# A four-stage block on one core: the delta rule's iteration is cut into other pieces, its triangle formed one iteration ahead, and Exp and Ln share one table set in stage one

## The reference

```
# stage one, the parts that use exp and ln
delta = softplus(delta @ W_dt.T + b_dt);  deltaA = exp(delta[..., None] * -exp(A_log))
# stage three: 8 heads of 32, chunks of 32 tokens, for each batch, head and chunk:
q, k, v = silu(causal_conv4(x @ W));  q, k = l2norm(q), l2norm(k);  beta = sigmoid(x @ b_w)
attn = strict_lower(-(k * beta) @ k.T)
for i in range(1, 32):                        # the triangular solve
    attn[i, :i] += attn[i] @ attn[:, :i]
attn += I;  u = attn @ (v * beta);  w = attn @ (k * beta)
# the chain over the chunks, S is the 32x32 state of a head
u = u - w @ S;  o = q @ S + lower(q @ k.T) @ u;  S = S + k.T @ u
```

## Time and profile before

| | us |
|---|---|
| median of three runs (lowest, highest) | 2549.03 (2548.79, 2552.73) |
| the profiled execution | 2558.99 |
| its span, first to last instruction | 2557.4 |
| stage one, about | 0 to 1111 |
| stage three, first to last DVE instruction | 1384.5 to 2291.1 |

### The profile page before, as it was taken

One profiled execution on the slowest core, in us unless ns is written; L12 is line 12 of the kernel. 1 busy time (PEld: TensorE's weight loads), 2 busy tenths in 40 slices (PEclk: granted clock), 3 DMA queues, 4 the chain that ended last, 5 costly groups with the idle time before them and its releaser, 6 DMA issues. The chain is left out here.

```text
span 2557.4 us, 33988 instructions
## 1 busy us (share of the span) xinstructions
PE 1259.5 (49%) x13656; PEld 592.4 (23%) x13656; DVE 1503.6 (59%) x1992; ACT 915.0 (36%) x1547; POOL 979.6 (38%) x447
## 2 busy tenths in 40 slices
PE   4455555555555554336553343454543535354654
PEld 1112121212121211013221112233322233332222
DVE  1688888888979787943112356456464554625112
ACT  4574747564656565412101231332313313012110
POOL 0788787878787887910000000101101011020000
PEclk8667777776667776558775665676766757567776
DMA  3717171717171717058983001111121110218995
GB/s 91 164 42 181 42 181 42 181 43 181 43 181 43 169 42 169 17 196 300 382 335 104 17 25 43 27 34 26 38 55 26 34 31 22 59 50 312 355 389 196
DMA packets 205726, 311.13 MB, mean 122 GB/s; under 512 B 84944, under 2 KB 136912, under 8 KB 189200
## 3 DMA queue, kind: packets, MB, share of 16 engines
q1 hardware_dynamic: 202512, 306.54, 40.6%
q0 software_dynamic: 2048, 2.10, 0.4%
q10 hardware_dynamic: 1024, 0.53, 0.1%
HBM read 266.12 MB, written 42.99 MB: 121 GB/s over the span
## 5 line engine op out<-in xcount | busy, mean ns | idle before, releaser
L347 POOL TENSOR_TENSOR state<-dx_rep,b_rep 128x2048 f32<-128x2048 f32 x128 | 577.6, 4524 | 64.0 <-issue 49.6
L557 DVE TENSOR_TENSOR_SCAN psum<-psum,state 128x1024 f32<-128x1024 f32 x160 | 365.9, 2287 | 97.1 <-ACT psum L446 61.2
L687 PE MATMUL psum<-state,sel 128*32 128x512 f32 x1024 | 191.3, 835 | 347.8 <-POOL state L354 339.3
L446 ACT ACTIVATE psum<-delta_rep,a_neg 128x511 f32<-128x511 f32 x512 | 330.4, 680 | 67.3 <-DVE state L557 67.0
L354 POOL TENSOR_TENSOR state<-state,c_rep 128x1024 f32<-128x1024 f32 x96 | 225.7, 2351 | 126.8 <-DVE state L557 126.8
L557 DVE TENSOR_TENSOR_SCAN state<-psum,state 128x1024 f32<-128x1024 f32 x96 | 218.7, 2278 | 18.3 <-ACT psum L446 18.3
L623 PE MATMUL psum<-xt,w_in 128*128 128x512 f32 x256 | 178.9, 863 | 82.9 <-DVE delta L532 44.3
L564 DVE TENSOR_TENSOR state<-psum,c_rep 128x1024 f32<-128x1024 f32 x160 | 195.9, 1224 | 5.5
L1457 DVE TENSOR_TENSOR prod<-t_lane,n_lane 128x1 f32<-128x1 f32 (+30 forms) x248 | 134.2, 541 | 82.5 <-DMA n_lane<-n_scratch 75.2
L832 POOL DMA_DIRECT2D moe_b<-in_w x64 | 33.3, 522 | 324.1 <-DVE moe_xt L962 320.2
L1642 PE MATMUL psum<-xt_delta,w_qkv 128*128 128x512 f32 x192 | 116.5, 762 | 60.2 <-DVE conv_qkv L1445 58.8
(11 more groups left out here) (191 smaller groups left out, 2312.4 us busy)
## 6 DMA issues: line engine op xcount, KB each, us to landing
moe_w_set<-in_w SPq DMA_DIRECT2D x32, 4096.0 KB, 36.1
delta_rep<-delta_scratch SPq DMA_DIRECT2D x128, 256.0 KB, 4.5
dx_rep<-dx_scratch SPq DMA_DIRECT2D x128, 256.0 KB, 7.3
moe_x<-x_after SPq DMA_DIRECT2D x32, 512.0 KB, 8.5
b_rep<-bc_scratch SPq DMA_DIRECT2D x32, 256.0 KB, 4.8
c_rep<-bc_scratch SPq DMA_DIRECT2D x32, 256.0 KB, 7.7
delta_scratch<-delta SPq DMA_DIRECT2D x32, 256.0 KB, 2.0
dx_scratch<-delta_x SPq DMA_DIRECT2D x32, 256.0 KB, 2.4
```

Of the source, the lines that this page charges most:

```text
L347: nc.gpsimd.tensor_tensor(ring[q % RING][:, :, :], dx_rep[u % CHUNKS][:, :, :], free_bcast(b_rep[q // QPB % 2][:, g, :], 1, CB), ALU.mult) ...
L446: ins = nc.scalar.activation(dec[:, i, 1:], delta_rep[u % CHUNKS][:, c, 1:], ACT.Exp, scale=a_neg[:, dt * CB + c, g:g + 1])
L557: nc.vector.tensor_tensor_scan(bx if by_pool(k) else flat, flat, bx, 0.0, ALU.mult, ALU.add).then_inc(S["scan_done"], 1)
L687: ins = nc.tensor.matmul(bank[32 * c:32 * c + 32, :], sel[:, :], ring[q % RING][:, c, :], start=False, stop=(g == NG4 - 1), skip_group_che ...
```

## The change

In stage one ACT loads the set "natural_log_exp_and_others", which holds both Exp and Ln, ahead of `norm_root` and after each group of Silu. ACT_TABLE_LOADs in the program's list for stage one go from 78 to 33, in stage three from 33 to 17.

In stage three front is split: *conv* (unit i+2: layer norm, transposes, projections, taps) and *front* (unit i+1: Silu, statistics, gates, tokens, gram). An iteration has 16 slots and takes pieces of five stages, so of up to five units, before four; there are 12 iterations instead of 11. The triangles of a unit are formed in slots 6 to 8 of the iteration before their solve; `n_lane` and `t_lane` have two copies each. The solve's rows are spread over slots 0 to 14, conv's taps stand in slots 11, 13 and 15, the chain in slots 4 to 15. v has one buffer of its own, and all Silu of a unit stand together in slot 0. POOL scales the solved triangle in slot 3 of the iteration in which the chain reads it. SP stores the triangles ahead of the tail's store.

```diff
@@ -447,6 +447,7 @@
                                                    scale=a_neg[:, dt * CB + c, g:g + 1])
                     ins.then_inc(S["decay_ready"], 1)
 
+                nc.scalar.preload_act_table_set("natural_log_exp_and_others")
@@ -498,6 +502,7 @@
                         if i == 29:
                             z_silu(n, 2)
                             z_silu(n, 3)
+                            nc.scalar.preload_act_table_set("natural_log_exp_and_others")
...
-    SLOTS = 3 * CT
+    SLOTS = 4 + 3 * CT
-        cuts = [1, 14, 18, 22, 25, 28, C]
-        return range(cuts[m], cuts[m + 1]) if m < 6 else ()
+        cuts = [1, 9, 13, 16, 19, 21, 23, 24, 25, 26, 27, 28, 29, 30, 31, C, C]
+        return range(cuts[m], cuts[m + 1])
...
+        feats = [m_.sb(f"feat{i}", P, 2 * KD, CT, P) for i in range(COPIES)]
+        v_feat = m_.sb("v_feat", P, KD, CT, P)
...
-        n_lane = m_.sb("n_lane", P, C, C)
-        t_lane = m_.sb("t_lane", P, C, C)
+        n_lanes = [m_.sb(f"n_lane{i}", P, C, C) for i in range(2)]
+        t_lanes = [m_.sb(f"t_lane{i}", P, C, C) for i in range(2)]
...
         def iterations(iteration):
-            for i in range(-1, NU + 2):
-                iteration(i, front=i + 1 if i + 1 < NU else None, solve=i if 0 <= i < NU else None,
-                          chain=i - 1 if 0 <= i - 1 < NU else None, tail=i - 2 if 0 <= i - 2 else None)
+            unit = lambda w: w if 0 <= w < NU else None
+            for i in range(-2, NU + 2):
+                iteration(conv=unit(i + 2), front=unit(i + 1), solve=unit(i), chain=unit(i - 1), tail=unit(i - 2))
...
-                    if front is not None and front + 1 < NU:
-                        load_x(front + 1)
+                    if front is not None:
+                        sp.wait_ge(S["n_read"], HS * (front + 1))
+                        for p in range(NP):
+                            sp.dma_start(n_scratch[front, 32 * p:32 * p + 32, :, :].rearrange("l i j -> i l j"),
+                                         n_tok[32 * p:32 * p + 32, :, :, :].rearrange("i n h j -> i (n h) j")).then_inc(
+                                S["n_stored"], 16)
+                        sp.wait_ge(S["n_stored"], 64 * (front + 1))
+                        if front >= 2:
+                            sp.wait_ge(S["solve"], SOLVE * (front - 1))
+                        sp.dma_start(n_lanes[front % 2][:, :, :].rearrange("l i j -> l (i j)"),
+                                     n_scratch[front].rearrange("l i j -> l (i j)")).then_inc(S[f"n_loaded{front % 2}"], 16)
+                    if conv is not None and conv + 1 < NU:
+                        load_x(conv + 1)
                     if tail is not None:
                         sp.wait_ge(S["out_added"], 2 * (tail + 1))
...
-                    if front is not None:
-                        sp.wait_ge(S["n_read"], HS * (front + 1))
...
-                        sp.wait_ge(S["n_stored"], 64 * (front + 1))
-                        if front:
-                            sp.wait_ge(S["solve"], SOLVE * front)
-                        sp.dma_start(n_lane[:, :, :].rearrange("l i j -> l (i j)"),
-                                     n_scratch[front].rearrange("l i j -> l (i j)")).then_inc(S["n_loaded"], 16)
...
-                        if front is not None and m == 3 and f:
+                        if conv and m == 9:
...
-                        if solve is not None and m == 8:
-                        if front is not None and m == 9:
+                        if chain is not None and m == 3:
+                            t_tok = t_toks[chain % 2]
+                            pool.wait_ge(S[f"t_loaded{chain % 2}"], 64 * (chain // 2 + 1))
...
-                        if front is not None and m == 11:
+                        if front is not None and m == 6:
...
+                        if front is not None and m == 0:
+                            feat = feats[f % COPIES]
+                            act.wait_ge(S["conv_done"], NT * (f + 1))
+                            for t in range(2 * KD):
+                                ins = nc.scalar.activation(tokens_by_chunk(feat, t), by_chunk(raw, t), ACT.Silu)
+                            ins.then_inc(S["qk_feat"], 1)
+                            if f:
+                                act.wait_ge(S["tok_psum"], CT * f)
+                            for t in range(KD):
+                                ins = nc.scalar.activation(tokens_by_chunk(v_feat, t), by_chunk(raw, 2 * KD + t), ACT.Silu)
+                            ins.then_inc(S["v_feat"], 1)
+                            nc.scalar.preload_act_table_set("natural_log_exp_and_others")
+                            act.wait_ge(S["qk_feat"], f + 1)
+                            if f:
+                                act.wait_ge(S["stat_psum"], f)
+                            nc.scalar.activation(squares[:, :, :], feat[:, :, :, :].rearrange("c t n l -> c t (n l)"),
+                                                 ACT.Square).then_inc(S["sq_ready"], 1)
+                        if tail is not None and m == 1:
...
-                        if m == 6:
-                            act.wait_ge(S["carry"], f + 1)
-                            last_tap(f, 0)
-                            last_tap(f, 1)
-                        if m == 7:
-                            last_tap(f, 2)
-                            last_tap(f, 3)
...
+                        if conv is not None and m in (11, 13, 15):
+                            if m == 11:
+                                act.wait_ge(S["carry"], a + 1)
+                            last_tap(a, m - 11)
+                            last_tap(a, m - 10)
...
                     if i == 1:
-                        dve.wait_ge(S["n_loaded"], 16 * s + 16)
+                        dve.wait_ge(S[f"n_loaded{s % 2}"], 16 * (s // 2 + 1))
                         if s:
-                            dve.wait_ge(S["t_stored"], 16 * s)
+                            ch.wait()
+                        if s >= 2:
+                            dve.wait_ge(S["t_stored"], 16 * (s - 1))
                     else:
                         ch.wait()
+                    n_lane, t_lane = n_lanes[s % 2], t_lanes[s % 2]
...
-                            if m == SLOTS - 1:
-                                read_o(k)
+                        if tail is not None and m == 0:
+                            read_o(CT * tail + CT - 1)
+                        if conv is not None and m == 0:
+                            dve.wait_ge(S["x_loaded"], 64 * (a + 1))
...
-                        if m == 11:
-                            dve.wait_ge(S["lam_mask"], f + 1)
-                            if f:
-                                dve.wait_ge(S["n_stored"], 64 * f)
-                            for g in range(HS):
-                                mask_gram(f, g)
+                        if front is not None and m in (7, 8):
+                            if m == 7:
+                                dve.wait_ge(S["lam_mask"], f + 1)
+                                if f:
+                                    dve.wait_ge(S["n_stored"], 64 * f)
+                            mask_gram(f, 2 * (m - 7))
+                            mask_gram(f, 2 * (m - 7) + 1)
+                        if tail is not None and m == 9:
+                            dve.wait_ge(S["res_loaded"], 64 * (tail + 1))
...
+                        if conv is not None and m in (11, 13, 15):
+                            taps(a, (m - 11, m - 10))
...
                         pe.wait_ge(S["v_feat"], f + 1)
-                        pe.wait_ge(S["qk_feat"], f + 1)
+                        pe.wait_ge(S["stat_ready"], f + 1)
+                        pe.wait_ge(S["gate_exp"], f + 1)
+                        pe.wait_ge(S["ssq_ln"], f + 1)
                     else:
...
-                        if tail is not None and m == 2:
+                        if front is not None:
+                            if m == 1:
+                                statistics(f)
+                            if m == 3:
+                                statistics_to_tokens(f)
+                            if m == 5:
+                                for n in range(CT):
+                                    to_tokens(f, n)
+                            if m == 6:
+                                gram(f, 0)
+                            if m == 7:
+                                gram(f, 1)
+                        if tail is not None and m == 8:
+                            grams = HS * NU if front is None else HS * (f + 1)
...
-                        if tail is not None and m == 3:
+                        if tail is not None and m == 9:
...
-                        if m == 4:
-                            pe.wait_ge(S["ln_done"], f + 1)
-                            if f:
-                                pe.wait_ge(S["n_read"], HS * f)
-                                pe.wait_ge(S["attn_read"], HS * f)
```

(26 more changed lines are left out.)

209 lines of the change are left out of this document (83 added, 126 removed).

## The result

The changed kernel takes **2341.81 us** (median of 4 runs, 2340.74 to 2348.64), the kernel before, beside it, 2548.91 (4 runs). The ratio is 0.9196, 95% interval 0.9176 to 0.9216. The forecast was 2344.

A forecast was written before the change was run, and what follows sets the result against it. DVE nearly saturated in stage one; in stage three no engine full, the period being front latency plus the solve on DVE. 2559.0 - 40 - 165 = 2354, less 10 gives 2344 us; 8 in 10 range 2290 to 2402.

The forecast's parts named there:

- Stage one, -40: Stage one: removed ACT table loads shorten DVE's waits, 35 us over 7 batches plus 5.1 before the first scan.
- POOL did not take ACT's place: Stage one, rival: every wait on ACT turns into one on POOL and nothing is gained; 2384 us, 6%.
- The bound of 48: Stage one's upper end: the whole of the 2.39 and 4.92 waits goes, less a little.
- Experts, 0: Expert stages: they keep their code and their work, so 0 change.
- profiled run, -10: Whole kernel: the profiled execution of before is 10.0 us above the median of three, so 10 is taken off.
- The period, 85: Stage three, full iteration: DVE work 62.2 plus waits 19.5 is 81.7, with 3 for POOL contention 85, against 106.4.
- Port contention, +3: Stage three's solve: five more DVE products lengthened by POOL operations, up to 6.7 us per iteration, 3 taken after absorption.
- Fill and drain: Stage three's first and last iterations beside the full ones: 12 iterations sum to 742 against 906.6, giving -165 us.
- PE at full clock throughout: Stage three, rival: PE runs at 2.4 GHz and never holds DVE up for long; period 74, 2284 us, 10%.
- GpSimd paid in full: Stage three, rival: POOL's operations cost their full time and PE's own stalls add; period 95, 2402 us, 14%.
- The round trips in every slot: Stage three, PE's queue in slots 4 to 15, rival: every slot a PE-DVE round trip, slower than before; 2%.
- rival 5: Stage three: solve still tied to its own period by the stored triangle's wait or one buffer; second copies remove both; 1%.

The follow-up runs named there:

- stage one alone: The kernel before with only stage one's five table loads by name: 2508.9 us, ratio 0.9835; DVE's waits on POOL in stage one 26.5.
- the kernel with short GpSimd products: The kernel after with five of the six large GpSimd products per stage-three iteration cut to a quarter of their columns: 2321.7 us, ratio 0.9093.
- the memsets: The kernel after with six added GpSimd memsets of a 128x704 scratch tile per solve, beside rows 26 to 31: 2346.6 us, ratio 0.9197.
- the multiplication by a constant: The kernel after with six added GpSimd multiplications by 1.0 of a 128x704 scratch tile per solve, beside rows 26 to 31: 2338.8 us, ratio 0.9166.
- the kernel with the early rows: The kernel after with the solve's 31 rows all in slots 0 to 5, triangles still formed one iteration ahead: 2430.1 us, ratio 0.9524.
- the kernel with one buffer each: The kernel after with one buffer for the loaded triangles and one for the solved ones: 2346.6 us, ratio 0.9202.
- the gram part: The kernel after with PE's second gram pair behind t times y of chunk 1 and the tail's transposes one slot later: 2352.8 us, ratio 0.9230.

## Why the prediction was right, step by step

- **Stage one, -40**: 39.7. The wait of 2.62 stayed, 2.39 went, 4.92 became 2.15 (2.3 forecast); waits on ACT 40.6 in all (about 36 forecast). POOL did not take ACT's place, as stage one alone showed. The bound of 48 was added up too low: 7 x (2.39 + 4.92) and the 5.1 before the first scan are 56.
- **Experts, 0; profiled run, -10**: the unchanged expert stages were 3.6 and 4.6 us shorter in the profiled run of after. That is 8 of the 10 by which the profiled run of before stood above its median, so the -10 was the right term for it.
- **The period, 85**: 85.5, 87.4, 86.1, 81.8. Four full ones were put at 338 and took 340.9. The walk named every place where DVE waits: y of chunk 0 1.4 (1.60 in the iteration at 1737.8), y of chunk 1 2.3 (1.81), masks 0.4 (0.89), state of chunk 0 0.5 (none), state of chunk 1 3.1 (5.20), residual 0.9 (1.21), y of chunk 2 3.1 (1.85), taps 2.8 (1.81), y of chunk 3 2.1 (2.83), state of chunk 3 2.9 (4.61); 19.5 against 21.8 in all. Mis-sized were the two states: gram 1, t times y, q times state and the tail's transposes stand in front of k times u, and I had given t times y no gap of its own; and the projection pairs two and three were put at 5 us. That y of chunk 2 and the taps came out shorter than forecast made up for part of it. PE's rows of the three pairs in after:
```profile
1798.35 3.70 PE L1636 MATMUL psum<-xt_delta,w_qkv 128*128 128x512 f32 x8 [0.15 <-ACT xt_delta L1421]
...
1808.16 5.99 PE L1636 MATMUL psum<-xt_delta,w_qkv 128*128 128x512 f32 x8 [3.60 <-DVE conv_qkv L1446]
...
1821.02 6.38 PE L1636 MATMUL psum<-xt_delta,w_qkv 128*128 128x512 f32 x8 [4.34 <-DVE conv_qkv L1446]
```
  After an idle time of 3.6 and 4.3 us, in which PE waits for DVE's taps, a pair takes 6.0 and 6.4 us at a granted clock of 0.61 and 0.57, where the first pair, which follows PE's work, takes 3.7 at 1.00.
- **Port contention, +3**: right in size, wrong in its picture, and so right in part by luck. I expected five more products at up to 1.34, 6.7 in all, each ending when GpSimd ends, with more than half absorbed by waits. DVE's work rose from 60.1 to 62.5 per iteration, and the kernel with short GpSimd products shows that almost nothing was absorbed. Three products and the layer norm's shift, a tiny operation with two SBUF inputs, are held, and a held product only *starts* then. In the earlier trace rows too the product ends 0.35 behind POOL's, which I read as the same time. After:
```profile
1760.09 2.06 POOL L1311 TENSOR_TENSOR t_tok<-t_tok,lam 128x1024 f32<-128x1024 f32 x1
...
1770.81 1.91 POOL L1325 TENSOR_TENSOR lam_mask<-lam,neg_strict 128x1024 f32<-128x1024 f32 x1
```
```profile
1760.72 1.45 DVE L1521 SCALAR_TENSOR_TENSOR neg_mean_rstd_delta<-mean_var_delta,rstd_delta 128x4 f32<-128x4 f32 x1
...
1771.42 1.82 DVE L1461 TENSOR_TENSOR prod<-t_lane,n_lane 128x484 f32<-128x484 f32 x1
```
  The mask product ends at 1772.72; DVE's, normally 0.66, ends at 1773.24, so it started about 0.14 before the other's end. The shift, normally 0.15, started 0.13 before the end of `t_tok`. Over the iteration the lengthening is 0.7 + 1.2 + 1.2 + 1.3, about 4.3, against the 1.34 of the one product before: 3.0 more. The two GpSimd products with v held nothing in this iteration: beside the first DVE wrote the new state from PSUM, in its usual 1.28, and the second started behind a product of DVE and was itself lengthened to 2.41. The Trainium skill's rule (SBUF — State Buffer, "SBUF: two separate sides") that a two-input operation is blocked only by one that reads SBUF is borne out by the memsets, which a running product did not hold up. Its "for the whole instruction" is borne out for GpSimd's products with two inputs, not for the multiplication by a constant: 0.65 of 1.97.
- **Fill and drain**: the sum's iterations begin at slot 0, where row 1 stands, so they are compared by the distances from row 1 to row 1 in the table above. First solve at 96.8 after the stage's start (101), third iteration 64.6 (60), fourth 73.5 (77), the four full ones 339.3 (338), the one without conv 59.6 (60), all that follows 103.4 (46 + 60 = 106). No term is off by more than 5 us, and the errors, of both signs, come to 737.3 against 742.
- **Rivals**: PE at full clock throughout did not come (0.72 to 0.75, period 86). GpSimd paid in full (95) did not. The round trips in every slot (121) did not, but the kernel with the early rows shows what that rival was about: with the same work for PE, a full period is 93 instead of 85 on average when no rows stand between the chain's pieces. That ACT's 16 removed loads gain nothing in stage three was not tried by itself.
- **Wrongly credited**: where rival 5 says that the second copies free the solve from its own period, the kernel with one buffer each shows that they do not: the full iterations are as short without them. What is left as the reason is that the triangles are formed in the iteration before.

## What to carry to other kernels

When two in-order engines hand work back and forth, find for each stretch which of them is late, and move the other's independent pieces there. Reordering an engine's queue where it is late renamed the wait here; it won 12 us where that engine stood idle for the other one with the chain's piece queued behind. Look at the iterations that fill and drain the pipeline apart from the full ones: the gram part and the single buffers cost nothing in the full ones and 8 and 4 us in the last, and the early rows lost more in the partial ones than in the full ones. Measure a period between two places that stand in the same slot in both kernels. Price the second buffer by what already stands between its last reader and the next writer.

## What the runs showed of the hardware

A GpSimd memset of 128x704 took 0.69 and was not held up by a running product of DVE; a GpSimd multiplication of the same tile by a constant took 1.97, held up the products that started in its first 0.65 and none that started at 1.15 or later, and was itself stretched to 2.75 by a product already running. A DVE operation of 4 columns with two SBUF inputs took 1.45 instead of 0.15 beside a GpSimd product: what is held is the start, which came 0.13 us before the other's end, as for the product of 484 columns (0.14). A projection pair took 3.70 at a granted clock of 1.00 and 5.99 and 6.38 at 0.61 and 0.57, when PE had been idle for 3.6 and 4.3 us before it.
